# A two-stage convolution kernel on one core: the second stage's products, sums and final additions in another order over two granules, tap weights in six groups

## The reference

```python
t = jax.nn.relu(group_norm(d4_1x1(x, w1), gn_gamma, gn_beta, cmid))
tr = t.reshape(b, cmid, 8, h, w)
wgt = jnp.einsum('oi,bighw->boghw', w2, tr) + b2[None, :, None, None, None]
...
xv = d4_1x1(x, w_v)
pats = unfold_patches(xv, k).reshape(b, G, gc, 8, k * k, h, w)
out = (wv * pats).sum(axis=4)
...
x = x + _L1_conv_ref(_gn(x), ...)
```

## Time and profile before

| what | value |
|---|---|
| median of 3 runs | 5366.03 us (5357.07 to 5376.06) |
| the profiled execution: time / span | 5362.72 / 5360.9 us |
| PE matmul busy | 4678.5 us (87%) |
| DVE busy | 3950.6 us (74%) |
| POOL busy | 3903.2 us (73%) |
| ACT busy | 2911.8 us (54%) |
| the DMA queue's packets | 41.7% of 16 engines' span |
| mean granted TensorE clock | 0.951 |

### The profile page before, as it was taken

The page is one execution under the profiler, slowest core; times in us unless marked ns, Lnnn a source line. Parts: engine busy times, 40 slices in busy tenths (PEclk is TensorE's granted clock), DMA queues, the critical chain, the costliest instruction groups (busy, mean ns, idle before and its releaser), DMA issues.

```text
span 5360.9 us, 147175 instructions
## 1 busy us (share of the span) xinstructions
PE 4678.5 (87%) x53372; PEld 1923.4 (36%) x53372; DVE 3950.6 (74%) x6113; ACT 2911.8 (54%) x4802; POOL 3903.2 (73%) x1953
## 2 busy tenths in 40 slices
PE   8999999979898989898979798989888888888865
PEld 3333333313333333333333333333333333333333
DVE  6777777726777777677777777777777777687877
ACT  7999999945454444444544444444444444445321
POOL 6788887806777767676767776777777777677777
PEclk9999999989999999999989898999999999999987
DMA  8999999832232323232323232323232323232222
GB/s 238 256 257 257 256 258 256 214 104 94 88 112 81 112 85 115 84 116 84 115 87 113 86 110 85 111 88 108 88 108 88 108 89 106 93 107 94 94 68 72
DMA packets 889309, 681.45 MB, mean 127 GB/s; under 512 B 576464, under 2 KB 839120, under 8 KB 872272
## 3 DMA queue, kind: packets, MB, share of 16 engines
q1 hardware_dynamic: 888656, 672.82, 41.7%
HBM read 404.18 MB, written 268.44 MB: 125 GB/s over the span
## 4 chain that ended last, share of the span: by engine, by line
PE 52%; DVE 9%; issue 7%; POOL 6%; ACT 5%; DVEq 0%; POOLq 0%; ACTq 0%; DMA 0%; SPq 0%
PE ps L833 17%; PE ps L771 11%; PE ps L799 8%; PE ps L812 7%; POOL sum_p L1128 6%; PE ps L786 5%; PE ps L761 4%; DVE prod_p L1154 4%; DVE prod_d L1154 3%; ACT xh L936 3%; DVE six_t L1143 2%; ACT t L1029 1%; ACT ps L1024 1%; DVE acc L1190 0%; ACT val L1018 0%
## 5 line engine op out<-in xcount | busy, mean ns | idle before, releaser
L1128 POOL TENSOR_TENSOR sum_p<-sum_p,prod_p 128x1024 f32<-128x1024 f32 x1280 | 3041.4, 2376 | 1087.9 <-DVE prod_p L1154 1009.9
L1154 DVE TENSOR_TENSOR prod_p<-ps,val 128x1024 f32<-128x1024 f32 x1280 | 1514.6, 1217 | 86.0 <-ACT ps L1024 86.0
L833 PE MATMUL ps<-prod_d,base 64*64 64x256 f32 x12288 | 867.7, 417 | 426.4 <-POOL sum_p L1128 256.7
L1190 DVE TENSOR_TENSOR acc<-ps,acc 128x512 f32<-128x512 f32 x512 | 353.6, 691 | 923.9 <-PE ps L833 922.7
L293 PE MATMUL ps<-xn,band 64*64 64x512 f32 x8192 | 948.0, 598 | 22.9 <-issue 15.5
L1154 DVE TENSOR_TENSOR prod_d<-ps,val 128x1024 f32<-128x1024 f32 x768 | 889.5, 1215 | 20.2 <-issue 17.2
L833 PEld LDWEIGHTS ps<-prod_d,base 64*64 64x64 f32 x12288 | 475.3, 143 | 839.3 <-issue 729.1
L771 PE MATMUL ps<-xh,wh 128*32 128x512 f32 x6144 | 708.2, 600 | 9.6 <-DVE wh L1235 9.6
L1018 ACT ACTIVATE val<-ps 128x512 f32<-128x512 f32 (+1 forms) x640 | 349.5, 557 | 574.1 <-PE ps L799 566.5
L325 POOL TENSOR_TENSOR x_out<-x_out,x_in 128x512 f32<-128x512 f32 x512 | 636.1, 1275 | 0.0
L253 ACT ACTIVATE x_out<-ps 64x512 f32<-64x512 f32 x1024 | 607.1, 593 | 50.4 <-PE ps L293 30.2
(11 more groups left out here) (69 smaller groups left out, 3335.3 us busy)
## 6 DMA issues: line engine op xcount, KB each, us to landing
x_in<-x SPq DMA_DIRECT2D x128, 1024.0 KB, 7.4
x<-x_out SPq DMA_DIRECT2D x256, 512.0 KB, 5.4
xr<-x SPq DMA_DIRECT2D x512, 256.0 KB, 3.3
acc<-x SPq DMA_DIRECT2D x2048, 64.0 KB, 1.9
out<-acc SPq DMA_DIRECT2D x256, 512.0 KB, 2.7
prod_p<-wsrc SPq DMA_DIRECT2D x1, 384.0 KB, 4.9
w<-w2t SPq DMA_DIRECT2D x1, 288.0 KB, 4.8
shift_m<-shifts SPq DMA_DIRECT2D x1, 256.0 KB, 5.8
```

Of the source, the lines that this page charges most:

```text
L833: mm = nc.tensor.matmul(ps[to:to + H2, SUM_BANKS[1 - t], UPX:], same[rows, :], term[rows, at:at + UPX], start=(j == 0), stop=(j == len(ter ...
L1128: nc.gpsimd.tensor_tensor(total, total, prod_p[:, k % P_RING, :], ALU.add).then_inc(p_added, 1)
L1154: return nc.vector.tensor_tensor(dst.rearrange("p (m r w) -> p m r w", m=count, w=W), taps_of(tap).rearrange("p (m r w) -> p m r w", m=1, ...
```

## The change

The nine taps are put into other PSUM half banks in six groups instead of five: tap 2 alone in bank 4, taps 0 and 1 in bank 0, 3 and 4 in bank 1, 5 in bank 2, 6 in bank 5, 7 and 8 in bank 3.

- DVE (`granule`) makes pooled products 0, 1 and 2 of granule n + 1 already in step n: 0 and 1 between the two final additions, 2 (which now starts `sum_p`) after them. In step n + 1 products 3, 4, 5 follow the direct ones of granule n and stand before the final addition.
- POOL adds products 0, 1, 3, 4, 5 to product 2.
- PE and ACT: in steps 3, 7, 11 and 15 three taps are renewed at the start and three at the end of the step, in steps 0, 4, 8 and 12 one at the start and two after the first sums. `inverse` stands before `forward`. `block_v` stands before the second sums. Both chunks 6 and 7 of `block_v` are in step 13. The values of the next image's granule 0 are made in step 14, of granule 1 between the sums of step 15. `t_affine` and the first `relu` move to step 14.

```diff
-TAP_BANKS = {0: (0, 1), 1: (2, 3), 4: (5,), 2: (4, 6), 3: (7, 8)}
+FIRST_P, SUM_P, LAST_P = (0, 1), 2, (3, 4, 5)
+TAP_BANKS = {4: (2,), 0: (0, 1), 1: (3, 4), 2: (5,), 5: (6,), 3: (7, 8)}
...
-BLOCK_V_AT = {1: 0, 2: 1, 4: 2, 5: 3, 8: 4, 9: 5, 13: 6, 14: 7}
+BLOCK_V_AT = {1: (0,), 2: (1,), 4: (2,), 5: (3,), 8: (4,), 9: (5,), 13: (6, 7)}
...
-MOMENTS_AT, EDGES_AT = 14, 14
-RSTD_AT = (14, 2)
+MOMENTS_AT, EDGES_AT = 14, 13
+RSTD_AT = (14, 3)
@@ sums (PE)
-                if n % GRANS == GRANS - 1 and n < N_GRAN - 1:
-                    wait_apart(pe, pe_apart, tap_ready, tap_count(i, (n + 1) // GRANS, 4))
+                if (n + 1) % GRANS == GRANS - 1 and (more or n + 2 < N_GRAN):
+                    wait_apart(pe, pe_apart, tap_ready, tap_count(i, (n + 2) // GRANS, 4))
+                if (n + 1) % GRANS == 0 and n + 1 < N_GRAN:
+                    wait_apart(pe, pe_apart, tap_ready, tap_count(i, (n + 1) // GRANS, 5))
@@ period (PE; ACT's is changed in the same way)
+                ahead = n % GRANS == GRANS - 1 and (more or n < N_GRAN - 1)
+                after = (i, u + 1) if n < N_GRAN - 1 else (i + 1, 0)
+                if ahead:
+                    tap_weights(*after, TAP_ORDER[:2])
                 if n % GRANS == 0:
-                    tap_weights(i, u, TAP_ORDER[2:4])
+                    tap_weights(i, u, TAP_ORDER[4:5])
                 if more and n == MOMENTS_AT:
                     means(i + 1)
-                if more and n in FORWARD_AT:
-                    forward(i + 1, FORWARD_AT[n])
                 if more:
                     for c in INVERSE_AT.get(n, ()):
                         inverse(i + 1, c)
+                if more and n in FORWARD_AT:
+                    forward(i + 1, FORWARD_AT[n])
                 if not (begin and n == 0):
-                    sums(i, n - 1, 0)
+                    sums(i, n - 1, 0, more)
                 if more and n == MOMENTS_AT:
                     variances(i + 1)
+                    pe.wait_ge(xm_edges, EDGES * (i + 2))
+                    values(0)
...
                 if more and n == N_GRAN - 1:
-                    pe.wait_ge(xm_edges, EDGES * (i + 2))
-                    values(0)
+                    values(1)
+                if more:
+                    for c in BLOCK_V_AT.get(n, ()):
+                        block_v(i + 1, c)
                 if not (begin and n == 0):
                     sums(i, n - 1, 1)
                 if more:
-                    if n in BLOCK_V_AT:
-                        block_v(i + 1, BLOCK_V_AT[n])
                     for c in BLOCK_T_AT.get(n, ()):
                         block_t(i + 1, c)
-                if n % GRANS == GRANS - 1 and n < N_GRAN - 1:
-                    tap_weights(i, u + 1, TAP_ORDER[:2])
                 if more and n == N_GRAN - 1:
-                    values(1)
-                    tap_weights(i + 1, 0, TAP_ORDER[:1])
                     values(2)
-                    tap_weights(i + 1, 0, TAP_ORDER[1:2])
+                if ahead:
+                    tap_weights(*after, TAP_ORDER[2:4])
@@ period (POOL)
-                for j in range(1, NP):
-                    k = NA * n + j - 1
-                    pool.wait_ge(*p_done(i, n, j))
+                for a, j in enumerate(FIRST_P + LAST_P):
+                    k = NA * n + a
+                    pool.wait_ge(*p_done(i, n, max(j, SUM_P)))
@@ granule (DVE)
+        def opening(i, n, more):
+            img, m = (i, n) if n < N_GRAN else (i + 1, n - N_GRAN)
+            dve.wait_ge(kept, values_end(img, m, more))
+            if m >= GRANS:
+                dve.wait_ge(halo_ready, halo_count(img, m))
+            for j in FIRST_P:
+                pooled(img, m, j)
+
         def granule(i, n, more, begin=False):
             if not begin:
                 for j in range(ND):
                     direct(i, n - 1, j)
-            pooled(i, n, 0)
-            pooled(i, n, 1)
-            pooled(i, n, 2)
+            for j in LAST_P:
+                pooled(i, n, j)
             if not begin:
                 final(i, n - 1, 0)
-            pooled(i, n, 3)
-            pooled(i, n, 4)
+            if more or n + 1 < N_GRAN:
+                opening(i, n + 1, more)
             if not begin:
                 final(i, n - 1, 1)
-            pooled(i, n, 5)
+            if n + 1 < N_GRAN:
+                pooled(i, n + 1, SUM_P)
+            elif more:
+                pooled(i + 1, 0, SUM_P)
```

More of the change, by code:

```diff
@@ L540, in order_of_period @@
                     yield ("means", 0), 1
+                for c in INVERSE_AT.get(n, ()):
+                    yield ("inverse", c), MT
                 if n in FORWARD_AT:
                     yield ("forward", FORWARD_AT[n]), IRR
-                for c in INVERSE_AT.get(n, ()):
-                    yield ("inverse", c), MT
                 if n == MOMENTS_AT:
@@ L817, in tap_weights, with sums @@
                 mm.then_inc(tap_mm, 1)
-        def sums(i, n, half):
+        def sums(i, n, half, more=True):
             if half == 0:
@@ L1061, in period @@
                 u = n // GRANS
+                ahead = n % GRANS == GRANS - 1 and (more or n < N_GRAN - 1)
+                after = (i, u + 1) if n < N_GRAN - 1 else (i + 1, 0)
+                if ahead:
+                    tap_bias(*after, TAP_ORDER[:2])
                 if n % GRANS == 0:
-                    tap_bias(i, u, TAP_ORDER[2:4])
+                    tap_bias(i, u, TAP_ORDER[4:5])
                 if more and n == MOMENTS_AT:
                     keep_means(i + 1)
-                if more and n in FORWARD_AT:
-                    keep_forward(i + 1, FORWARD_AT[n])
                 if more:
@@ L1070, in period @@
                         keep_inverse(i + 1, c)
+                if more and n in FORWARD_AT:
+                    keep_forward(i + 1, FORWARD_AT[n])
+                if n == 0:
+                    relu(i, 3)
                 if more and n == MOMENTS_AT:
                     keep_variances(i + 1)
-                if n == 0:
-                    relu(i, 3)
+                    keep_values(i + 1, 0)
+                    t_affine(i + 1)
+                    relu(i + 1, 0)
                 if n % GRANS == 0:
-                    tap_bias(i, u, TAP_ORDER[4:])
+                    tap_bias(i, u, TAP_ORDER[5:])
                 if n + AHEAD < N_GRAN:
@@ L1079, in period @@
                 if more and n == N_GRAN - 1:
-                    t_affine(i + 1)
-                    relu(i + 1, 0)
-                    keep_values(i + 1, 0)
+                    keep_values(i + 1, 1)
+                    relu(i + 1, 1)
                 if more:
-                    if n in BLOCK_V_AT:
-                        keep_block_v(i + 1, BLOCK_V_AT[n])
+                    for c in BLOCK_V_AT.get(n, ()):
+                        keep_block_v(i + 1, c)
+                    if n == EDGES_AT:
+                        edges(i + 1)
                     for c in BLOCK_T_AT.get(n, ()):
                         keep_block_t(i + 1, c)
[L1088 to L1091, removed]
                 if more and n == N_GRAN - 1:
-                    keep_values(i + 1, 1)
-                    tap_bias(i + 1, 0, TAP_ORDER[:1])
-                    relu(i + 1, 1)
                     keep_values(i + 1, 2)
-                    tap_bias(i + 1, 0, TAP_ORDER[1:2])
                     relu(i + 1, 2)
+                if ahead:
+                    tap_bias(*after, TAP_ORDER[2:4])
         period(0)
@@ L1159, in tap_wait @@
         def tap_wait(i, n, tap):
-            if n % GRANS == 0 and tap == TAP_BANKS[bank_of(tap)][0] or tap == D_TAPS[0] and n % GRANS == 0:
+            if n % GRANS == 0 and tap == TAP_BANKS[bank_of(tap)][0]:
                 dve.wait_ge(tap_ready, tap_count(i, n // GRANS, bank_of(tap)))
```

20 lines of the change are left out of this document (9 added, 11 removed).

## The result

The changed kernel takes 5474.81 us (median of 4 runs, 5471.65 to 5476.13) against 5368.81 for the kernel before (4 runs). The ratio is 1.0199, with a 95% interval of 1.0179 to 1.0218. The prediction was 5336 with a range to 5400, so it was wrong in sign and in size. The profiled execution has a span of 5472.0 us, 111.1 more than before.

What follows compares the result with a forecast made beforehand. Order of work bounds it: PE's work in heavy steps, DVE's chain in light ones. 5362.7 profiled, -20 for 15 images, -10 for the last, gives 5333; the median is 3.3 above: 5336 us, range 5283 to 5400.

Steps and rivals of the forecast that it cites:

- The two kinds of step: Stage B: heavy steps last as long as PE's work, 17.04 us; in light steps DVE's chain decides.
- DVE's chain of 7.78: Light steps: final addition, one product and three direct products, 7.78 us from second sums to next first sums.
- the sum: Gains and losses of one image added up: -4.1 us without more cold clock, -1.3 with it.
- Step 13's loss: Step 13: from 13.88 to 19.94 us, as eight block_v outputs precede the second sums; loss 6.1.
- `inverse` behind `block_t`: Steps 1, 4, 5, 8, 9: inverse waits for ACT's copies, 0.80 us each less rounding; loss 3.9 per image.
- The last image: Its 16 steps, bound by POOL before, gain 0.6 us each: -10 us.
- Gain 14.1: Steps 14 and 15 together: from 46.74 to 32.7 us, the largest gain per image.
- its gap of 2.31 and a like one after it: PE between steps 15 and 0: both gaps were to go with the queue of values and taps, within the 14.1.
- the clock's price: First sums of steps 8 and 12 at the low clock: 1.4 us each, +2.8 per image.
- 0.7 for 14: Steps 14 and 15: 0.7 us added for values that run partly cold, giving 32.7.
- The slower rival: Clock falls in steps 4, 8, 12 and over 14's values: 9.6 instead of 3.5 per image, 5428 us; chance 0.17.
- 10.16: Light steps with statistics: DVE's chain of 7.78 plus 2.38 us, from second sums to next first sums.

Runs made afterwards that it cites:

- the experiment with `block_v`: The changed kernel with block_v put back behind the second sums on PE; 5307.1 us, ratio to before 0.989.

## Why the prediction was wrong

**Right.** The two kinds of step (PE's sum of work, or DVE's chain of 7.78) describe the changed kernel too: steps 1, 5, 9, 13 and 0 came within 0.2 us. POOL left the chain, and it had been worth little outside step 14, whose gain the sum had. Step 13's loss (6.1 predicted, 6.15 measured) was right, and the experiment with `block_v` showed its cause. `inverse` behind `block_t` costs 0.72 in a heavy step, and I had 0.80. The last image gave 14.8 where I had 10, and that is luck of the clock: the same instructions gave 6.4 in the run with `block_v` put back and 6.8 in the one with the statistics moved too.

**The step that failed first: "Gain 14.1" at the boundary.** Steps 14 and 15 together went from 46.66 to 37.25, a gain of 9.4. The failed words are "what goes is the queue of values and taps between steps 15 and 0, with its gap of 2.31 and a like one after it". The like one after it is the jump of PE's loop. It stayed and grew from 2.4 to 2.8, and PE's next work comes behind it at a low clock. In step 15 of the changed kernel the gap of 2.8 and a `forward` of 5.6 instead of 4.0 make 4.4 of the missing 4.7. Taking only PE's jump away gives back 3.1, because ACT's jump then holds `forward`; in the kernel before it gives back 3.8. The evidence was in the trace of before, where the last boundary has no such gap, since PE leaves the loop there. The taps of a boundary inside the loop and of the last one:

```profile
2257.83 4.28 PE L812 MATMUL ps<-t,w 128*32 128x256 f32 x48 [2.44 <-DVE prod_p L1154]
...
5116.68 5.08 PE L812 MATMUL ps<-t,w 128*32 128x256 f32 x80
```

In the first the taps are parted, 48 of the 80 matmuls behind the gap; in the last they run on. An image came out 8.4 longer and not 1.3 shorter, 9.7 apart, and this step is 4.7 of it.

**The step that failed second: the clock's price.** I took 2.8 us per image for steps 8 and 12 and 0.7 for 14. By the table X after, less the full-clock values (9.07, 9.07 and 5.5), it is 1.6 in step 4, 3.1 in step 8 and 1.7 in step 12; 0.47 each in steps 4 and 8 is a wait for ACT (below), which leaves 1.2, 2.6 and 1.7. In step 6 the three taps at the start of step 7 cost 1.2 more in the mean. That is 6.7 instead of 2.8, another 3.9 per image. I priced the sums alone. The low clock went on into the taps and the values behind them, and it also fell after shorter gaps that the sum priced at nothing. Before the three taps at the start of step 7 PE waits 1.94 us in every image, and in 9 of 13 the taps then took 4.15 to 4.48 instead of 2.80. The first sums of step 4, after a gap of 2.0, were slow in 9 of 13 too. The slower rival named this mechanism with 9.6 per image and was given 0.17. The Trainium skill, TensorE: Matmul & The Clock Gate, The HAM clock gate, says that activity releases the throttle. By that rule work added in the gap should help, and the trace agrees: with the gap filled the first sums of step 8 were fast in 10 of 13 images and the kernel was 54 us faster.

**What was left out.** In steps 3, 7, 10 and 11 the first sums that follow have one wait more, for the bias of a tap, and PE starts them 0.88 us after DVE's last direct product. At the first sums of step 1, from which I took the chain of 7.78, it is 0.54. That adds about 0.35 in each of the four, also where the bias had been done for over 1 us; what takes the time is not shown. It is not new in all of them: the kernel before has 10.49 from S1 to S0 in step 11 (2180.11 to 2190.60), where I wrote 10.16. And ACT's copies of the values hold `block_v` for 0.47 in steps 4 and 8, a wait that no row of before could show. Together this is 2.3 per image. The three causes make 10.9 against the 9.7; small steps in the other direction and the accuracy of the means lie between.

**Only argued.** How much of the gain that remains belongs to DVE's and POOL's early products and how much to the moved values was not taken apart. The early taps and the loop were changed in one run. That ACT's gap at the boundary is its own jump is read from its place in the traces and was not tested by a run. And in which images the clock falls after the same gap is not explained by any row here.

## What to carry to other kernels

Write an in-order schedule as alternating stretches between two engines, and put a third engine's work into the stretch in which its consumer is not waiting. `block_v` cost nothing behind the second sums and 6 us in front of them, with the same instructions. Before booking a gap as a saving, look for the same place outside the loop: if the gap is missing there, it is the loop's own. Two cheap edits found on the way paid in the unchanged kernel too, statistics moved to steps 8 and 12, 0.7%, though mostly by where the low clock then fell, and fewer jumps, 0.6%.

## What the hardware showed that I had not expected

Where PE's loop jumps back it idles for 2.6 to 3.1 us in the changed kernel and 1.9 to 3.5 in the kernel before, and without the jump step 15 is 3.1 and 3.8 us shorter. Once the profile calls the gap "issue" and once it names a product of DVE. In the place of ACT's jump there is a gap of 1.3 to 1.9 us that shows only when PE's is gone. What within a jump takes the time is not shown. A gap of 1.94 us on PE was followed by slow matmuls in 9 of 13 images and by fast ones in four. And work added to an idle PE made the kernel 54 us faster, because the clock did not fall to its lower level.
